# Four residual graph layers on one core: the convolution's first slots moved in the instruction order, and psi's bias written by ScalarE

## The reference

```
layer 0 (attention):  A = exp(8*tanh((x@q)@(x@k).T / sqrt(128) / 8)) * adj;  A /= rowsum(A);  out = A@x@v
layer 1 (gated, 5 steps):  m = adj@h;  av = [m, m];  u3 = h@u3_w.T + u3_b
      z = sigmoid(av@w3_w.T + w3_b + u3);  r = sigmoid(av@w4_w.T + w4_b + u3)
      hv = tanh(av@w5_w.T + w5_b + (r*h)@u5_w.T + u5_b);  h = (1-z)*h + z*hv
layer 2 (Chebyshev):  x@W0 + sum over k=1..3 of adj^k @ x @ (W_k + W_{k+3})
layer 3 (messages):   f = relu(x@psi_w + psi_b);  msg = (adj*adj).T @ f
      out = relu([msg, x]@phi1_w + phi1_b) @ phi2_w + phi2_b
```

## Time and profile before

| what | value |
|---|---|
| time, median of 3 runs | 1312.88 us (1312.2 to 1313.59) |
| the profiled execution | 1311.03 us |
| its span, first to last instruction | 1309.2 us |
| PE, PEld busy | 97%, 87% of the span |
| DVE, POOL, ACT busy | 81%, 78%, 75% |
| mean granted TensorE clock | 0.994 of full speed |

### The profile page before, as it was taken

One profiled execution on the slowest core, in us unless ns is written; L12 is line 12 of the kernel. 1 busy time (PEld: TensorE's weight loads), 2 busy tenths in 40 slices (PEclk: granted clock), 3 DMA queues, 4 the chain that ended last, 5 costly groups with the idle time before them and its releaser, 6 DMA issues.

```text
span 1309.2 us, 27304 instructions
## 1 busy us (share of the span) xinstructions
PE 1270.0 (97%) x8126; PEld 1134.5 (87%) x8126; DVE 1066.5 (81%) x2522; ACT 979.3 (75%) x1767; POOL 1019.4 (78%) x1019
## 2 busy tenths in 40 slices
PE   8999989999999999999999999998799999999997
PEld 7999977888888888888888888886589999999996
DVE  4788877888888888888888888888688888888886
ACT  4788878778788787887877888877456777777774
POOL 5988888888888888888888888888456666666654
PEclk9999999999999999999999999999999999999999
DMA  3233332533323533324334223342033222222211
GB/s 111 82 98 108 102 114 71 150 86 81 97 56 83 151 81 88 82 62 140 93 88 98 59 71 87 88 128 82 19 96 89 73 71 70 71 68 74 71 33 41
DMA packets 143005, 111.71 MB, mean 85 GB/s; under 512 B 13906, under 2 KB 114132, under 8 KB 142932
## 3 DMA queue, kind: packets, MB, share of 16 engines
q1 hardware_dynamic: 142500, 110.68, 31.5%
q10 hardware_dynamic: 432, 0.20, 0.1%
HBM read 60.49 MB, written 50.33 MB: 85 GB/s over the span
## 4 chain that ended last, share of the span: by engine, by line
PE 86%; DVE 4%; POOL 4%; issue 3%; ACT 2%; DMA 1%; SPq 0%; POOLq 0%; ACTq 0%; DVEq 0%
PE psum L1296 6%; PE psum L855 5%; PE psum L857 5%; PE psum L383 4%; PE psum L1308 3%; PE psum L1310 3%; PE psum L898 3%; PE psum L899 3%; PE psum L900 3%; PE psum L875 3%; PE psum L870 3%; PE psum L887 3%; PE psum L874 3%; PE psum L869 3%; PE psum L888 3%
## 5 line engine op out<-in xcount | busy, mean ns | idle before, releaser
L790 POOL TENSOR_TENSOR rh_lo<-rh,rh_hi 128x512 fp32r<-128x512 f32 x160 | 207.5, 1297 | 40.2 <-ACT rh_hi L949 40.0
L797 POOL TENSOR_TENSOR h_lo<-h,h_hi 128x512 fp32r<-128x512 f32 x160 | 209.5, 1309 | 11.5 <-ACT h_hi L922 1.7
L970 DVE TENSOR_TENSOR psum<-psum,h 128x512 f32<-128x512 f32 x160 | 111.9, 699 | 103.5 <-ACT psum L953 103.5
L855 PE MATMUL psum<-adj_t_hi,hn_hi 128*128 128x256 f32 x640 | 161.4, 287 | 4.0 <-DVE m_lo L986 4.0
L936 ACT ACTIVATE psum<-psum,bias_cols 128x512 f32<-128x512 f32 x160 | 106.2, 664 | 76.6 <-PE psum L875 74.7
L857 PE MATMUL psum<-adj_t_hi,hn_lo 128*128 128x256 f32 x640 | 156.8, 280 | 0.0
L804 POOL TENSOR_TENSOR hn_lo<-hn,hn_hi 128x512 fp32r<-128x512 f32 x96 | 124.0, 1292 | 37.4 <-ACT hn_hi L944 37.4
L949 ACT CAST rh_hi<-rh 128x512 fp32r<-128x512 f32 x160 | 99.6, 623 | 71.1 <-DVE rh L992 71.1
L855 PEld LDWEIGHTS psum<-adj_t_hi,hn_hi 128*128 128x128 f32 x640 | 120.9, 189 | 9.6 <-issue 5.1
L857 PEld LDWEIGHTS psum<-adj_t_hi,hn_lo 128*128 128x128 f32 x640 | 120.6, 188 | 4.4
L986 DVE TENSOR_TENSOR m_lo<-psum,m_hi 128x512 fp32r<-128x512 f32 x160 | 108.7, 679 | 10.9 <-ACT m_hi L931 10.9
(11 more groups left out here) (277 smaller groups left out, 4323.9 us busy)
## 6 DMA issues: line engine op xcount, KB each, us to landing
h_dram<-squares SPq DMA_DIRECT2D x512, 64.0 KB, 1.8
hn<-h_dram SPq DMA_DIRECT2D x96, 256.0 KB, 2.7
x_in<-in_x_dram SPq DMA_DIRECT2D x32, 256.0 KB, 3.0
x_dram<-x SPq DMA_DIRECT2D x32, 256.0 KB, 2.1
g_x<-x_dram SPq DMA_DIRECT2D x32, 256.0 KB, 4.7
ht<-h_dram SPq DMA_DIRECT2D x32, 256.0 KB, 2.8
c_x<-x_dram SPq DMA_DIRECT2D x32, 256.0 KB, 3.0
out_dram<-res SPq DMA_DIRECT2D x32, 256.0 KB, 2.4
```

The source lines that it names most:

```text
L790: pool.tensor_tensor(rh_lo[:, q, :], rh[:, q, :], rh_hi[:, q, :].bitcast(F32), ALU.subtract).then_inc(rh_lo_done, 1)
L797: pool.tensor_tensor(h_lo[:, q, :], h[:, (g - 1) % G, :], h_hi[:, q, :].bitcast(F32), ALU.subtract).then_inc(h_lo_done, 1)
L855: pe.matmul(dst, hn_hi[:, p, tile(b, c), :], adj_hi[:, c, :], start=(b == 0 and c == 0), stop=False, skip_group_check=True)
L970: dve.tensor_tensor(cb, cb, hg, ALU.subtract).then_inc(dif_done, 1)
```

## The change

It has two parts. **The order**: the lists given to `weave` get new numbers, and to make them possible the gated layer writes out its last sixteen slots instead of eight, and its SyncE program yields at the moves of two steps. VectorE's convolution slot becomes two pieces, `slot` and `sum_with_x2` (`y2` with its moments). **The bias**: ScalarE writes psi's bias into bank `B_F` from a new tile `psi_b`, right behind `x3t`, and the matmul L1334 goes. The two waits of the first loads on stored `h` are split to fit.

```diff
-  for _ in weave(both, conv["sync"](sp), [150, 156, 159, 164, 166, 168, 170]):
+  for _ in weave(both, conv["sync"](sp), [142, 152, 156, 164, 165, 166, 168]):
-  for _ in weave(both, conv["gpsimd"](pool), [152, 153, 155, 159, 162]):
+  for _ in weave(both, conv["gpsimd"](pool), [145, 146, 150, 157, 162]):
-  for _ in weave(both, conv["tensor"](pe), [154, 158, 162]):
+  for _ in weave(both, conv["tensor"](pe), [149, 154, 162]):
-  for _ in weave(both, conv["scalar"](act), [154, 156, 158, 160, 162]):
+  for _ in weave(both, conv["scalar"](act), [149, 151, 155, 158, 162]):
-  for _ in weave(both, conv["vector"](dve), [154, 158, 162, 165, 167, 169, 171]):
+  for _ in weave(both, conv["vector"](dve), [149, 149, 156, 156, 162, 162, 163, 164, 164, 165, 165, 167, 167]):
...
+  sp.dma_start(env["psi_b"][:, :], t["L3_gnn_psi_b"].rearrange("(o d) -> o d", o=1).broadcast_to([128, D]))\
+    .then_inc(rest_loaded, 16)
-  sp.wait_ge(rest_loaded, 16 * 4)
+  sp.wait_ge(rest_loaded, 16 * 5)
...
-  with eng.Fori(G, SET_SLOTS - G, G) as at:
+  with eng.Fori(G, SET_SLOTS - 2 * G, G) as at:
-  for s in range(SLOTS - G, SLOTS + lags):
+  for s in range(SLOTS - 2 * G, SLOTS + lags):
...
-  if isinstance(it, int) and s == 8:
-      for g, done in enumerate(earlier["h_out"]):
-          sp.wait_ge(done, earlier["h_stored"][g % 4] * GROUPS // 8)
+  if isinstance(it, int) and s == 8:
+      for done, stored in zip(earlier["h_out"], earlier["h_stored"]):
+          sp.wait_ge(done, stored * (GROUPS // 8 - 1))
+  if not isinstance(it, int) and u == 1:
+      for done, stored in zip(earlier["h_out"], earlier["h_stored"]):
+          sp.wait_ge(done, stored * (GROUPS // 8))
...
   pe.wait_ge(x3t_done, m + 1)
-  wait_count(pe, hid_done, m)
-  pe.matmul(psum[:, B_F, :], ones[:, :], flat(psi_row[:, :, :]), start=True, stop=False, ...)
+  pe.wait_ge(bias_set, m + 1)
...
   act.copy(x3t[:, :], psum[:, B_T23, :]).then_inc(x3t_done, 1)
+  wait_count(act, hid_done, m)
+  act.copy(psum[:, B_F, :].rearrange("p (i d) -> p i d", d=D),
+           env["psi_b"][:, :].rearrange("p (o d) -> p o d", o=1).broadcast_to([128, TILES, D])).then_inc(bias_set, 1)
...
   dve.tensor_tensor(x2t_lo[:, q, :], psum[:, x2t_bank(it, n), :], x2t_hi[:, q, :].bitcast(F32), ALU.subtract)...
+  def sum_with_x2(it, u):
       if live(it, u, L_W):
           dve.wait_ge(a_mm[2], w + 1)
...
-  yield from run(dve, slot)
+  yield from run(dve, slot, sum_with_x2)
```

More of the change, by code:

```diff
@@ L82, in adj_resnorm_d4_kernel @@
         phi2_b = keep("phi2_b", [128, D])
+        psi_b = keep("psi_b", [128, D])
         env = dict(locals())
@@ L759, in sync @@
                 for g in MOVED:
-                    if k == SETS - 1 and at == final - G:
-                        yield SLOTS - G + g - 3
+                    if k == SETS - 1 and at >= final - 2 * G:
+                        yield k * SET_SLOTS + at + g + 5
                     move(k, at, g)
@@ L1020, in vector @@
                     slot(k * SET_SLOTS + at, g, k, at)
-                    if k == SETS - 1 and at == final:
-                        yield SLOTS - G + g
+                    if k == SETS - 1 and at >= final - G:
+                        yield k * SET_SLOTS + at + g
         for s in range(SLOTS, SLOTS + 4):
@@ L1031, in gated_layer @@
     sems = {"h_out": h_out, "hn_lo_done": hn_lo_done[0], "m_lo_done": m_lo_done, "z_done": z_done,
-            "rh_done": rh_done, "h_done": h_done, "slots": SLOTS, "h_stored": tuple(stored(0, SET_SLOTS - G, g) for g in range(4)), "pairs_end": SLOTS - G}
+            "rh_done": rh_done, "h_done": h_done, "slots": SLOTS, "h_stored": tuple(stored(0, SET_SLOTS - G, g) for g in range(G)), "pairs_end": SLOTS - SET_SLOTS + G + 4}
     return programs, (earlier, sems)
@@ L1145, in run @@
             slot(GROUPS // U, u)
+            if second is not None:
+                second(GROUPS // U, u)
     def live(it, u, lag):
@@ L1177, in load @@
             if isinstance(it, int) and s < 8:
[L1178 removed]
+                sp.wait_ge(earlier["h_out"][s], earlier["h_stored"][s])
             if isinstance(it, int) and s == 8:
[L1180 to L1181 removed]
+                for done, stored in zip(earlier["h_out"], earlier["h_stored"]):
[3 more added lines that the diff above has]
+                    sp.wait_ge(done, stored * (GROUPS // 8))
             sp.dma_start(ht[:, u % 2, :], h_dram[bass.ds(s, 1), :, :].rearrange("o p c -> (o p) c"))\
@@ L1505, in slot @@
                 act.copy(x3t[:, :], psum[:, B_T23, :]).then_inc(x3t_done, 1)
+                if isinstance(it, int) and m == 0:
+                    act.wait_ge(earlier["h_done"], GATED)
+                wait_count(act, hid_done, m)
+                act.copy(psum[:, B_F, :].rearrange("p (i d) -> p i d", d=D),
+                         env["psi_b"][:, :].rearrange("p (o d) -> p o d", o=1).broadcast_to([128, TILES, D]))\
+                   .then_inc(bias_set, 1)
             if live(it, u, L_W):
@@ L1668, in slot @@
                                   ALU.subtract).then_inc(x2t_lo_done, 1)
+        def sum_with_x2(it, u):
+            s = it * U + u
+            w = s - L_W
             if live(it, u, L_W):
```

2 lines of the change are left out of this document (1 added, 1 removed).

## The result

| | before | after |
|---|---|---|
| time, median of 6 runs each on one chip | 1312.83 us (1311.21 to 1313.59) | 1317.81 us (1316.07 to 1318.32) |
| the profiled execution | 1311.03 us | 1316.07 us |
| its span | 1309.2 us | 1314.3 us |
| mean granted TensorE clock | 0.994 | 0.992 |

What follows compares the result with a forecast made beforehand. TensorE was taken to bound it, busy 97% of the span and full in undisturbed gated and steady slots. Gains of 6.8 and losses of 8.7 made it 1.9 us slower, 1314.8 us from 1312.88, range 1306.5 to 1319.5.

Steps and rivals of the forecast that it cites:

- the likeliest case, no change: Whole kernel: a time within about 0.2%, 2.6 us, of before; chance 0.36, against slower 0.34 and faster 0.30.
- bias: Convolution slots: without the bias matmul on TensorE each gains 0.15 us, in 27 slots 4.0 us (bounds 1.4 and 6.2).
- `x2` of group 1 no longer ahead of the wait at 932.68: Ending gated slots: without this ScalarE piece ahead, the chain to `rh_lo` and TensorE's 1.75 us wait is 1.0 us earlier.
- `c_lo` ahead of the first pair: First convolution slots: transposes of groups 0 and 1 now stand behind the `c_lo` that TensorE awaits 3.38 us; 1.2 gained.
- third pair: First convolution slots: one transpose instead of the pair that delays `c_lo`, TensorE's loss 0.3 instead of 0.9; 0.6 gained.
- stores in slot 7, clock, load of group 8: Convolution slot 7: VectorE's transposes wait for stores, 6.4 lost; lower clock behind, 0.7; later load of group 8, 0.5.
- Rival 2: Convolution slot 7: the wait for the stores is not there, 6.4 + 0.7 + 0.5 come back; 1307.2 us, chance 0.15.
- rival 1: Convolution slots: the stores' wait is there but ScalarE's copy takes 0.75 us, the bias gives nothing; 1318.8 us, chance 0.18.
- The second chain: Steady convolution slot: VectorE's unbroken work into `c_lo`, ending 1105.58, limits the gain to 0.05 to 0.23 us, 0.15 taken.
- That load was late before too; now some 0.5 us more: Convolution ramp: SyncE is held by the stores of groups 6 and 7 before loading group 8; 0.5 us lost.
- I leave both: 0 (+-1): Gated slots: TensorE's stalls at VectorE's slots 0 and 1, 1.67 and 1.87 us, stay as they were behind 149 and 156.
- Rival 3: Gated slots absorb the spread pieces: waits of 1.67, 1.04 and 1.87 halve, the low clock goes; 1309.6 us, chance 0.17.

Runs made afterwards that it cites:

- own_buffers: The changed kernel with the transposes of groups 6 and 7 of the last set in buffers of their own (`rh`); 1319.24 us, ratio 1.0061.
- ahead_own: `own_buffers` with SyncE's loads of groups 7 and 8 issued one convolution slot earlier; 1308.85 us, ratio 0.9976.
- slot0_at_151: `ahead_own` with VectorE's convolution slot 0 behind gated slot 151 instead of 149, its GpSimd and ScalarE pieces two later; 1306.9 us, ratio 0.9957.
- residuals_early: Old order with ScalarE's bias, GpSimd's two residuals behind gated slots 145 and 146 instead of 152 and 153, their loads moved too; 1312.03 us in one run.
- late_old: The changed kernel with VectorE's pairs of transposes and SyncE's pieces from 163 on as before, early numbers new; 1310.15 us, ratio 0.9983.

## Why the prediction was right in its bounds and wrong in its middle

The time lies inside the range, 3 us above its middle forecast, and outside of what was called the likeliest case, no change. The sum has 1.9 us, the traces 4.9. By its steps:

| step | forecast | measured |
|---|---|---|
| bias | -4.0 | -3.0 |
| gated slots: residuals +0.4, slot 0 at 0, new place of `x2` of group 1 +0.7 | +1.1 | +1.7 |
| `x2` of group 1 no longer ahead of the wait at 932.68 | -1.0 | -0.9 |
| `c_lo` ahead of the first pair | -1.2 | -1.2 |
| behind it up to F0 | not in the sum | -1.1, of which the clock 0.9 |
| third pair | -0.6 | 0 |
| load of group 7 | not in the sum | +2.3 |
| stores in slot 7, clock, load of group 8 | +7.6 | +6.6 |
| offset between the executions | | +0.4 |

**Right: the wait for the stores.** The largest term came much as worked out: the buffer, the two waits ended by a DMA (3.9 us, I had about 5), `y2` 7.2 us later (6.5 forecast; 1.3 of the 7.2 were there at F3 already), TensorE waiting in slot 7, and a low clock behind it (0.83 from 1000 to 1020). That these waits are what costs is shown only together with the loads: taking them away alone gave nothing (`own_buffers`), taking them away once the loads were ahead gave 6.7. Rival 2 is out.

**Right: the chain that bounds the bias.** The copy takes 0.60 us (0.61 taken), in the steady slot the next matmul starts where TensorE wants it, and rival 1 falls. The second chain was read rightly from the earlier trace rows; the size was 0.12 a slot and not 0.15, and it counts in 25 slots and not in 27. That is the whole 1.0 us. The Trainium skill, ScalarE: Activation LUTs, section "Step-by-step: what each stage is for", has ScalarE write faster to PSUM than to SBUF; of that this trace shows nothing, 0.60 us into PSUM against 0.59 and 0.61 into SBUF.

**Failed: "That load was late before too; now some 0.5 us more".** I looked at where SyncE stands for group 8 and not at what else was moved past it. The transposes of groups 2 and 3 come 20 us later than before, at 978.31, and SyncE's new place for the load of group 7 is behind their stores: SyncE waits for the transposes, then come 3.8 us of issue. In before that load was issued 10 us ahead of the residual that needs it and had some 7 to spare. This is the 2.3 us that make most of the error. And the 0.5 for group 8 is right only as long as the stores' wait covers it. Without that wait the late loads cost 8.3 - 1.4 = 6.9 us from F3 to F4, of which about 2 are the longer load of `own_buffers`. The prediction also left out that this load stands behind the wait for the last stores to land (1.75 us from the last store's issue to it).

**Failed: "I leave both: 0 (+-1)"** for VectorE's slot 0. Its wait grew from 1.67 to 3.19, and the gated slots of `ahead_own` end 3.1 us later than those of `slot0_at_151`, with the same piece two slots on. Of these 1.1 are the wait; the rest comes with the clock, which I had priced only in slot 7. That the stage as a whole missed by only 0.6 is partly luck: before had a fall of its clock in 916 to 926 that after has not. The 0.4 for the residuals was too small, 0.7 to 0.9 measured (`residuals_early`). Rival 3 is out in its strong form: the waits at slots 0 and 1 of VectorE are 3.19 and 1.90 instead of 1.67 and 1.87.

**Right: two steps of the ramp; luck: the third.** The chain behind `x2` of group 1 is 0.9 us earlier (1.0 forecast), and the wait ahead of the second `spread` chain fell from 3.38 to 2.18, the 1.2 forecast. `late_old` shows the first by itself, 0.9 at the same matmul, with the old wait of 3.38 behind it. The 1.1 us that follow were not in the sum. The clock is 0.9 of them, and that isn't the order's doing: `ahead_own` has the same program up to F0, the same wait of 2.19, and a clock of 0.80 in 950 to 956 where after has 1.00, and its ramp gives 2.3. The other 0.2 are the bias matmul that no longer stands ahead of F0. The third pair gave nothing that F2 shows: the wait of 0.79 fell to 0.35 at 971.26, but at F2 TensorE waited 0.30 for the bias copy, and 0.72 again at 995.21, in slots where ScalarE is late.

## What to carry to other kernels

When a piece is moved in a hand-written order, list for every queue, the DMA queue first, what now stands ahead of each load: a load behind a store waits for the data of that store and for its issue (3.8 us for eight DMAs), here also for a wait that the program had placed behind its last store (1.75 us), and one that was ten us early becomes the limit. Two limits that end at about the same time hide each other: curing the buffers alone showed nothing (`own_buffers`, 8.3 us from F3 to F4 against 6.6), with the loads ahead it brought 6.7. A change in two parts is to be timed in its parts: here one gave 3 us and the other took 8. And where two executions are compared point by point, the clock of each stretch stands beside the difference: two kernels level at one point can be level because one of them had just run slow.

## What the runs showed of the hardware

**The clock after a wait.** The same wait is followed by a fall of the granted clock in one execution and by none in another, and by a longer or a shorter one. Behind 1.90 us at 914.98 after has 1.00 in 916 to 926, behind 1.89 at 913.98 `ahead_own`, with the same program there, has 0.83 in 910 to 920. Behind 3.19 at 878.11 after has 0.66 in 876 to 886, behind 3.20 `ahead_own` has 0.83. Behind 2.18 or 2.19 at the start of the second `spread` chain after has 1.00 in 950 to 956 and `ahead_own` 0.80. There the fall costs 0.9 us from that matmul to F0 (8.84 us in after, 9.71 in `ahead_own`). So near waits of about 2 us the program alone doesn't decide whether the clock falls.

**The same load takes unequal time.** From the issue of the second load DMA to GpSimd's start it was 3.1 us in after at 969.99, right behind four store DMAs, and at 1002.77, where the program had waited for all stores to land. It was 4.9 at 983.39, right behind eight store DMAs, but also 5.0 in `own_buffers` at 1002.82, behind the same wait for the stores. So the stores alone don't explain it, and the cause is open.
